# Last stage of an adaLN block on one core: operands turned by transposing transfers instead of TensorE

## What is computed

```python
x = x + ga * (out @ Wo.T + bo)
h = _layernorm(x) * (1 + cb) + sb
gate = fp4_linear(h, w_gate)
y = fp4_linear(h, w_up)
h = silu(gate) * y
x = x + gb * fp4_linear(h, w_down)
```

## Time and profile before

| | us |
|---|---|
| median of 3 runs (lowest, highest) | 3646.24 (3642.79, 3647.29) |
| the profiled execution, its own time | 3647.05 |
| its span, first to last instruction | 3645.2 |
| TensorE matmul busy | 3308.7 (91%) |
| VectorE busy | 2764.1 (76%) |
| POOL busy | 1512.2 (41%) |
| ScalarE busy | 1035.5 (28%) |

### The profile page before, as it was taken

The page is one execution under the profiler, slowest core; times in us unless marked ns, Lnnn a source line. Parts: engine busy times, 40 slices in busy tenths (PEclk is TensorE's granted clock), DMA queues, the critical chain, the costliest instruction groups (busy, mean ns, idle before and its releaser), DMA issues. The chain is left out here.

```text
span 3645.2 us, 50953 instructions
## 1 busy us (share of the span) xinstructions
PE 3308.7 (91%) x16784; PEld 1498.4 (41%) x16784; DVE 2764.1 (76%) x3797; ACT 1035.5 (28%) x1454; POOL 1512.2 (41%) x1311
## 2 busy tenths in 40 slices
PE   5999997036999999999986999999999999999998
PEld 2554553021323332333323555555555555555554
DVE  4677675975666666666645898989898989898986
ACT  1332331003555555555541111111111111111111
POOL 0332331004555555555533444444444444445442
PEclk8999998567999999999997999999999999999999
DMA  5656556102222222222212100010101010101000
GB/s 185 180 181 208 177 176 196 44 1 66 68 73 72 72 73 68 73 67 74 72 41 81 32 30 32 29 32 29 32 29 32 29 32 29 32 29 32 29 23 15
DMA packets 194398, 252.71 MB, mean 69 GB/s; under 512 B 58581, under 2 KB 114261, under 8 KB 193493
## 3 DMA queue, kind: packets, MB, share of 16 engines
q1 hardware_dynamic: 177944, 245.07, 21.6%
q0 software_dynamic: 16384, 6.76, 1.2%
HBM read 154.68 MB, written 97.04 MB: 69 GB/s over the span
## 5 line engine op out<-in xcount | busy, mean ns | idle before, releaser
L1038 DVE TENSOR_REDUCE top<-ps_max 128x1 f32<-128x1024 f32 (+1 forms) x512 | 618.5, 1219 | 340.9 <-PE ps_max L1171 340.8
L1117 ACT ACTIVATE p<-ps_exp,p_bias 128x820 f32<-128x820 f32 x512 | 483.0, 943 | 457.6 <-PE ps_exp L1197 457.6
L1208 PE MATMUL ps_out<-p,v_tok 128*33 128x410 f32 x2048 | 453.0, 521 | 0.0
L1007 POOL DMA_INDIRECT o_d<-o_rows,chosen x256 | 249.0, 973 | 446.6 <-DVE o_rows L1064 373.7
L1642 ACT ACTIVATE silu<-f_g 128x512 f32<-128x512 f32 (+1 forms) x192 | 107.8, 561 | 801.5 <-PE f_u L1711 801.5
L1171 PE MATMUL ps_max<-k_max,q_max 96*128 96x512 f16 (+1 forms) x1024 | 314.4, 389 | 1.1 <-DVE top L1038 0.8
L1197 PE MATMUL ps_exp<-q_exp,k_exp 98*128 98x410 f16 x1024 | 266.7, 342 | 44.7 <-ACT p L1117 44.7
L1711 PE MATMUL f_g<-gu,xT_lo 128*128 128x512 f16 (+1 forms) x768 | 278.3, 362 | 0.0
L1709 PE MATMUL f_g<-gu,xT_hi 128*128 128x512 f16 (+1 forms) x768 | 278.1, 362 | 0.0
L1710 PE MATMUL f_g<-gu,xT_hi 128*128 128x512 f16 (+1 forms) x768 | 278.1, 362 | 0.0
L1709 PE MATMUL f_u<-gu,xT_hi 128*128 128x512 f16 (+1 forms) x768 | 277.5, 361 | 0.0
(11 more groups left out here) (201 smaller groups left out, 6417.7 us busy)
## 6 DMA issues: line engine op xcount, KB each, us to landing
k_max<-k_d SPq DMA_DIRECT2D x192, 128.0 KB
k_exp<-k_d SPq DMA_DIRECT2D x192, 128.0 KB
...
```

The lines of the kernel that those rows point to most:

```text
L1007: pool.indirect_dma_start(o_rows, bass.IndirectOffsetOnAxis(ap=con["chosen"][0:n, t, h:h + 1], axis=0), o_rows_of[u][0:n, t, :], None).the ...
L1038: ve.tensor_reduce(top[0:rows_of(t), t, half:half + 1], ps_max[c % 2][0:rows_of(t), :, :].rearrange("p a n -> p (a n)"), AX.X, ALU.max, ne ...
L1117: act.activation(p32[k % PB][:, :, :], ps_exp[:, :, 0:NQ], ACT.Exp, bias=con["p_bias"][:, 0:1], scale=scale).then_inc(p_done, 1)
L1208: last = pe.matmul(ps_out[at:at + VCOLS, 0:NQ], v_tok[u][:, t, :], p32[k % PB][:, s, :], start=k == 0, stop=k == STEPS - 1)
```

## The change

In `feed_forward` all three turns leave TensorE. ScalarE and VectorE now split the untransposed rows in SBUF into high and low halves (`a_hi`, `a_lo`, `x_hi`, `x_lo`, `hid_hi`, `hid_lo`), and SP turns each half by a transposing transfer from SBUF to SBUF. These are six transfers a tile: 128x512 float16 twice for `a` and twice for `x`, 128x1408 twice for the hidden row. The two banks `f_t` are gone; `f_g` and `f_u` have three each, `silu` three buffers, `xT_hi` and `xT_lo` two. The front of a tile (projection, residual, moments, normalisation) runs two slots ahead of the gates where it ran one ahead. `bo` goes into a precomputed `ga_bo`, which POOL adds to x (`bias`), and `take_attention` multiplies by `ga`. The normalisation moves to ScalarE, with a third small POOL instruction (`shift`). On TensorE the projection comes first in a slot and `down` between the first and second gate part. On VectorE the moments of tile t+2 stand between `hidden(t, 1)` and `hidden(t, 2)`. POOL's order in a slot is `bias`, `scale_hidden`, `scale_h`, `result`, `residual`, `deviation`, `modulate`. The loop has one turn fewer and the tail four slots more.

```diff
+        ga_bo = m.sb("ga_bo", [P, B, D], F32)
...
+        a_hi = m.sb("a_hi", [P, D], F16)
+        a_lo = m.sb("a_lo", [P, D], F16)
...
+        x_hi = m.sb("x_hi", [P, D], F16)
+        x_lo = m.sb("x_lo", [P, D], F16)
+        xT_hi = [m.sb(f"xT_hi{u}", [P, KC, P], F16) for u in range(2)]
+        xT_lo = [m.sb(f"xT_lo{u}", [P, KC, P], F16) for u in range(2)]
+        s32 = [m.sb(f"silu{k}", [P, 512], F32) for k in range(NG)]
...
+        hid_hi = m.sb("hid_hi", [P, FF], F16)
+        hid_lo = m.sb("hid_lo", [P, FF], F16)
...
+        ps_g = [m.ps(f"f_g{k}", [P, 512]) for k in range(3)]
+        ps_u = [m.ps(f"f_u{k}", [P, 512]) for k in range(3)]
...
+                def turn_a(t):
+                    if has(t, -1):
+                        hold(sp, w_ready, t, sp_held)
+                    hold(sp, a_low, t + 1, sp_held)
+                    for src, dst in ((a_hi, aT_hi), (a_lo, aT_lo)):
+                        sp.dma_start_transpose(dst[:, :, :], src[:, :]).then_inc(a_turned, 16)
+
+                def turn_x(t, t4):
+                    u = t4 % 2
+                    if has(t, -2):
+                        hold(sp, g_ready, (t - 1) * NG, sp_held)
+                    hold(sp, x_low, t + 1, sp_held)
+                    for src, dst in ((x_hi, xT_hi[u]), (x_lo, xT_lo[u])):
+                        sp.dma_start_transpose(dst[:, :, :], src[:, :]).then_inc(x_turned, 16)
+
+                def turn_hidden(t):
+                    if has(t, -1):
+                        hold(sp, d_ready, t, sp_held)
+                    hold(sp, hid_low, t + 1, sp_held)
+                    for src, dst in ((hid_hi, hT_hi), (hid_lo, hT_lo)):
+                        sp.dma_start_transpose(dst[:, :, :], src[:, :]).then_inc(hid_turned, 16)
 
                 def store(t, t4):
...
+                def slot(t, t4, b2, b_z):
                     if has(t, 3):
-                        load_a(t + 3, t4 + 3)
-                    if has(t, -3):
-                        store(t - 3, t4 + 1)
+                        turn_a(t + 3)
+                        load(t + 3, t4 + 3)
+                    if has(t, 4):
+                        load_a(t + 4, t4 + 4)
+                    if has(t, 1):
+                        turn_x(t + 1, t4 + 1)
+                    if has(t, -1):
+                        turn_hidden(t - 1)
+                    if has(t, -2):
+                        store(t - 2, t4 + 2)
...
+                def low_of_a(t, t4):
+                    ve.wait_ge(a_high, t + 1)
+                    ve.scalar_tensor_tensor(out=a_lo[:, :], in0=a_in[t4 % 2][:, :], scalar=O_UP, in1=a_hi[:, :], op0=ALU.mult,
+                                            op1=ALU.subtract).then_inc(a_low, 1)
 
                 def low_of_x(t):
-                    ve.wait_ge(t_hi, turn1_at(t) + 1)
-                    ve.tensor_tensor(xT_lo[:, :, :], ps_t[0][:, :].rearrange("p (c n) -> p c n", n=P), xT_hi[:, :, :],
-                                     ALU.subtract).then_inc(t_lo, 1)
-
-                def low_of_a(t):
-                    ve.wait_ge(a_hi, t + 1)
-                    ve.scalar_tensor_tensor(out=aT_lo[:, :, :], in0=ps_w[:, :].rearrange("p (c n) -> p c n", n=P), scalar=O_UP,
...
+                def take_attention(t, b):
                     ve.wait_ge(w_ready, t + 1)
                     need(ve, x2_done, t)
-                    ve.scalar_tensor_tensor(out=y[:, :], in0=ps_w[:, :], scalar=1.0 / (W_UP * O_UP), in1=bo[:, :],
-                                            op0=ALU.mult, op1=ALU.add).then_inc(y_done, 1)
+                    ve.scalar_tensor_tensor(out=y[:, :], in0=ps_w[:, :], scalar=1.0 / (W_UP * O_UP), in1=vec["ga"][:, b, :],
...
+                def slot(t, t4, b2, b_z):
+                    if has(t, 3):
+                        low_of_a(t + 3, t4 + 3)
                     if has(t, -1):
                         hidden_add(t - 1)
-                    if has(t, 1):
-                        moments(t + 1, t4 + 1)
+                    if has(t, 2):
+                        take_attention(t + 2, b2)
                     if has(t, -1):
                         hidden_take(t - 1)
                     if has(t, 1):
-                        normalise(t + 1, t4 + 1)
+                        quantise_h(t + 1)
                     hidden(t, 0)
+                    if has(t, -1):
+                        low_of_hidden(t - 1)
+                    if has(t, 1):
+                        low_of_x(t + 1)
                     if has(t, -2):
-                        low_of_hidden(t - 2, 2)
+                        take_down(t - 2, b_z)
                     hidden(t, 1)
                     if has(t, 2):
-                        low_of_a(t + 2)
-                    if has(t, 1):
-                        quantise_h(t + 1)
+                        moments(t + 2, t4 + 2)
                     hidden(t, 2)
                     hidden_units(t)
-                    if has(t, -2):
...
-                def residual(t, t4, b):
-                    hold(pool, y_done, t + 1, pool_held)
-                    pool.tensor_tensor(y[:, :], y[:, :], vec["ga"][:, b, :], ALU.mult).then_inc(ga_done, 1)
-                    pool.wait_ge(ga_done, t + 1)
-                    pool.wait_ge(fx_in[t4 % 2], in_turn(t, t4))
+                pool.wait_ge(vec_in["ga"], 16)
+                pool.wait_ge(bo_in, 16)
+                for b in range(B):
+                    pool.tensor_tensor(ga_bo[:, b, :], vec["ga"][:, b, :], bo[:, :], ALU.mult).then_inc(gabo_done, 1)
+                pool.wait_ge(gabo_done, B)
+
+                def bias(t, t4, b):
+                    hold(pool, fx_in[t4 % 2], in_turn(t, t4), pool_held)
+                    pool.tensor_tensor(xt[t4 % 2][:, :], xt[t4 % 2][:, :], ga_bo[:, b, :], ALU.add).then_inc(xg_done, 1)
+
+                def residual(t, t4):
+                    hold(pool, xg_done, t + 1, pool_held)
+                    pool.wait_ge(y_done, t + 1)
                     need(pool, res_done, t - 3)
                     pool.tensor_tensor(x2[t4 % 4][:, :], xt[t4 % 2][:, :], y[:, :], ALU.add).then_inc(x2_done, 1)
 
+                def deviation(t):
+                    hold(pool, fmv_done, t + 1, pool_held)
+                    pool.tensor_scalar(rstd[:, :], mv[:, 1:2], EPS, None, ALU.add).then_inc(frs_done, 1)
+                    pool.wait_ge(frs_done, t * 3 + 1)
+                    pool.tensor_tensor(rstd[:, :], rstd[:, :], half[:, :], ALU.pow).then_inc(frs_done, 1)
+                    hold(pool, frs_done, t * 3 + 2, pool_held)
+                    pool.tensor_scalar(shift[:, :], mv[:, 0:1], rstd[:, 0:1], -1.0, ALU.mult, ALU.mult).then_inc(frs_done, 1)
+
                 def modulate(t, b):
-                    hold(pool, fmv_done, t + 1, pool_held)
-                    pool.tensor_scalar(rstd[:, :], mv[:, 1:2], EPS, None, ALU.add).then_inc(fve_done, 1)
-                    pool.wait_ge(fve_done, t + 1)
-                    pool.tensor_tensor(rstd[:, :], rstd[:, :], half[:, :], ALU.pow).then_inc(frs_done, 1)
                     hold(pool, fxh_done, t + 1, pool_held)
                     pool.tensor_tensor(h[:, :], h[:, :], vec["cb"][:, b, :], ALU.mult).then_inc(cb_done, 1)
                     hold(pool, cb_done, t + 1, pool_held)
...
-                def slot(t, t4, b1, b2, b_z):
-                    if has(t, -3):
-                        result(t - 3, t4 + 1)
-                    if has(t, 1):
-                        residual(t + 1, t4 + 1, b1)
-                        modulate(t + 1, b1)
+                    deviation(1)
+                    modulate(1, 0)
+
+                def slot(t, t4, b2, b_z):
+                    if has(t, 2):
+                        bias(t + 2, t4 + 2, b2)
                     if has(t, -1):
                         scale_hidden(t - 1)
                     if has(t, 1):
                         scale_h(t + 1)
+                    if has(t, -2):
+                        result(t - 2, t4 + 2)
+                    if has(t, 2):
+                        residual(t + 2, t4 + 2)
+                        deviation(t + 2)
+                        modulate(t + 2, b2)
...
+                def high_of_a(t, t4):
+                    act.wait_ge(fa_in[t4 % 2], in_turn(t, t4))
+                    need(act, a_turned, t * 32)
+                    act.activation(a_hi[:, :], a_in[t4 % 2][:, :], ACT.Copy, scale=O_UP).then_inc(a_high, 1)
+
+                def normalise(t, t4):
+                    act.wait_ge(frs_done, t * 3 + 3)
+                    act.activation(h[:, :], x2[t4 % 4][:, :], ACT.Identity, bias=shift[:, 0:1], scale=rstd[:, 0:1])\
+                       .then_inc(fxh_done, 1)
...
+                def slot(t, t4, b2, b_z):
+                    if has(t, 3):
+                        high_of_a(t + 3, t4 + 3)
                     gate(t, 0)
-                    if has(t, -2):
-                        high_of_hidden(t - 2, 2)
+                    if has(t, -1):
+                        high_of_hidden(t - 1)
```

(29 more changed lines are left out.)

254 lines of the change are left out of this document (95 added, 159 removed).

## The result

The changed kernel takes 3742.59 us (median of 4 runs, 3741.95 to 3744.45) against 3645.20 for the kernel before (4 runs beside it): a ratio of 1.0268, 95% interval 1.025 to 1.0286. It is 97 us slower; forecast were 105. The profiled execution took 3744.45 us, its span is 3742.6.

A forecast was written before the change was run, and what follows sets the result against it. TensorE bounds the kernel before; VectorE becomes the bound at 20.1 + 5.2 + 2.3, laid out as 27.75 us a tile, 1.70 more. 57 x 1.70 = 97, + 11 - 3 = +105: 3751 us, own range 3715 to 3795.

The forecast's parts named there:

- VectorE's own work: VectorE's instructions in one tile of the new order, without waits, take 20.1 us, under TensorE's 23.98 us of matmuls.
- The five items: Five places in a tile where VectorE instructions wait for POOL at SBUF, 0.4 to 2.05 us each, together 5.2 us.
- Rival A: VectorE's low parts (scalar_tensor_tensor, two SBUF operands) do not wait for POOL: 25.65 us a tile, 3621 us; chance 0.12.
- The round trip: VectorE's moments of tile t+2 wait 2.3 us for POOL's residual, queued behind POOL's result, which take_down frees.
- The three terms: Per tile on VectorE: 20.1 us of own work, 5.2 of waits for POOL, 2.3 of wait before the moments.
- the layout: One tile laid out in time with measured durations and POOL's port waits: 27.75 us, 1.70 more than before.
- The ends: First and last tiles: start 11 us longer (turns behind loads, POOL's ga_bo, turn chain), end 3 us shorter.
- The turns by transfer: SP's transposing transfers, 1.25 MB a tile: 5.7 us, at most 17; issues at most 19 us; hidden under 27.75.
- rival B: Transposing transfers slower than copies, over 0.73 us a block every tile waits: 3930 us at 50 GB/s, or 5500; chance 0.25.
- The clock: TensorE's clock falls after 3.8 us gaps; 5 us a tile at half speed makes 26.5 us, no cost.
- C: TensorE stays the bound with 23.98 us a tile, VectorE's 7.5 us of waits shrinking to 3.9: 3520 us; chance 0.03.
- D: Gain and losses cancel within 0.2%, VectorE at 26 us a tile: 3646 us; chance 0.05.

The follow-up runs named there:

- e3: Against the changed kernel, POOL's two modulation instructions work on one column in place of 512, output leaving modulation out: 3643.8 us, 25.89 us a tile.
- e5: Against the changed kernel, only VectorE's take_down is moved, to behind hidden(t, 0): 3678.9 us, 26.43 us a tile.
- e4: Against the changed kernel, both parts of x and the high part of a are turned twice, 9 transfers for 6: 3755.5 us, 27.56 a tile.
- e1: Against the changed kernel, only VectorE's take_down is moved, from behind low_of_x to behind hidden_take: 3705.2 us, 26.76 us a tile.
- e10: Against the changed kernel, e3 and e5 together, output leaving the modulation out: 3585.1 us, 24.77 us a tile.
- e7: Changed kernel's instructions reordered, TensorE's down product last in the slot, hidden_add right behind its units: 3577.6 us, 0.9812 of the kernel before.

## Why the prediction was right

**The bound.** VectorE became it. Shown by e3 and e5, which change nothing on TensorE and shorten the tile by what VectorE's own rows gain, and by e4, which delays TensorE's input by 2.6 us and leaves the steady tile as it was.

**VectorE's own work.** 20.1 us forecast; 27.55 - 5.12 - 2.25 = 20.2 measured.

**The waits for POOL.** The five items, forecast and measured: product 0.4, 0.60; `low_of_a` 1.05, 1.06; first tensor_scalar of `hidden_add` 1.06, 1.07; `quantise_h` 2.05, 1.89; `low_of_hidden` 0.6, 0.50. Together 5.2 and 5.1. Where each lay was right as well. Behind it stands the Trainium skill (SBUF — State Buffer, Who interferes with whom), by which a VectorE instruction with two SBUF inputs contends with a POOL instruction that reads SBUF. The trace agrees (`a_lo` ends 0.55 us after POOL's addition), and for scalar_tensor_tensor, which no row of before showed, the change and e3 show it. Rival A falls by the row `a_lo`, 1753 ns; the stage's first two, with POOL idle, take 0.69 us.

**The round trip.** 2.3 forecast, 2.25 measured, ended by the residual as said.

**The tile.** 27.75 forecast, 27.55 measured. The three terms as rounded in the text give 27.6; the layout's 27.75 was 0.2 too long, 11 us over 57 tiles.

**The ends.** 57 tiles at 1.50 us are 86 of the 97 us, so 11 lie at the ends, against 11 - 3 = 8. The first gates start at 1968.17 instead of 1951.95, 16 us later, not 11. The step missed is in the order: tile 2's turn of `a` stands in SP's queue behind the turn of `x`, and its projection stands ahead of the first gates. The turn of `x` is issued up to 1957.85 and so lands near 1960.4; TensorE begins that projection at 1963.08 and, at the 1.2 GHz level after a wait of 15 us, takes 5.1 us over it: 7.8 of the 16. So 8 for 11 at the ends is near by luck: the start was 5 us off, and where those came back was not followed.

**The turns by transfer.** Hidden, as forecast, and cheaper than every bound but in the first tile: issues of 1.2 to 1.8 us (at most 3.0 forecast; the first two took 3.3 and 4.3), 2.5 us to land for 128 KB, 3.8 for 352 KB. Seven more blocks of 128x128 take 1.3 us, 0.19 us a block; rival B began at 0.73. The 1309 ns that the Trainium skill (VectorE: DVE Perf Modes, The three transpose paths) gives for one block alone don't add up over a larger turn, so its 5160 us did not come. The 261 GB/s of the Trainium skill (DMA: Bandwidth & Descriptors, Latency and other measured facts) aren't reached: 224 KB more in 1.3 us are some 180 GB/s, and from 3000 to 3002 us, while the hidden row is turned, the transfers move 208 to 210. It did not matter.

**The clock.** Forecast was half speed for about 5 us a tile, at no cost. It was 2.9 to 6.0 us in 21 of 50 tiles, 1.6 us a tile in the mean, at no cost, until e1 moved a consumer close behind TensorE: there it cost a third of the gain, 0.40 of 1.19 us a tile.

**TensorE.** Its wait for the turned `x` was forecast as some 3.8 us a tile; it is 2.7, with 0.8 more lost to the clock. C and D needed shorter waits of VectorE; those were as long as laid out. e10 shows C's premise from the other side: with 2.8 of their 7.4 us gone, TensorE's own 24 us nearly show.

What stays open: whether the 0.6 us a tile left in e7 can be had. Small steps of POOL out of the way of VectorE's row of two-operand instructions would be the next thing to try; that was not tried. Also not tried was one turn back on TensorE.
